# Layer 1 of a four-layer block: the input projected once per pixel and read back in tiles, and two sets of banks for the spreads

## The reference

```python
x_proj = x_nhwc @ w_in + b_in                       # 64 -> 64 channels, per pixel
x1 = gelu(layernorm(depthwise_conv3x3(x)))
offset = x1 @ w_off + b_off                         # 4 groups x 9 taps x 2
mask = softmax((x1 @ w_mask + b_mask), per group over the 9 taps)
out = sum over taps of mask * bilinear_sample(zero_padded(x_proj), tap position + offset)
out = out @ w_out + b_out
y = batch_norm(out);  x = x + y * sigmoid(y)
```

## Time and profile before

| | us |
|---|---|
| median of 3 runs | 1361.74 (1361.45 to 1363.02) |
| the profiled execution, whole | 1360.48 |
| its span, first to last instruction | 1358.7 |
| window_weights, from its first operation to the first transpose | 108.1 to 176.0 |
| transposes of pair 0 | 176.0 to 185.0 |
| spread phase, pair 0 | 185.0 to 220.5 |
| sums phase, pair 0 | 220.5 to 242.8 |
| spread phase, pair 1 | 242.8 to 281.7 |
| sums phase, pair 1 | 281.7 to 299.9 |

### The profile page before, as it was taken

The page is one execution under the profiler, slowest core; times in us unless marked ns, Lnnn a source line. Parts: engine busy times, 40 slices in busy tenths (PEclk is TensorE's granted clock), DMA queues, the critical chain, the costliest instruction groups (busy, mean ns, idle before and its releaser), DMA issues. The chain is left out here.

```text
span 1358.7 us, 31661 instructions
## 1 busy us (share of the span) xinstructions
PE 1114.5 (82%) x13352; PEld 602.8 (44%) x13352; DVE 890.2 (66%) x1220; ACT 645.3 (47%) x1096; POOL 663.2 (49%) x503
## 2 busy tenths in 40 slices
PE   3970099978859999999999576799999999998658
PEld 2440077754315666666666333233333333334323
DVE  3788945566956666667666379646666666667623
ACT  1656035353636677677666343144444444445410
POOL 2000011103345767767764330188888888888600
PEclk9985599898958999999999799699999999999869
DMA  4100000001234555555554005000000000002002
GB/s 87 23 1 0 0 3 3 1 11 43 53 112 141 166 156 163 164 155 160 169 155 117 2 0 140 1 1 2 1 1 2 2 1 2 1 2 80 1 18 71
DMA packets 41841, 75.15 MB, mean 55 GB/s; under 512 B 20876, under 2 KB 26093, under 8 KB 40925
## 3 DMA queue, kind: packets, MB, share of 16 engines
q1 hardware_dynamic: 41533, 72.77, 18.9%
q10 hardware_dynamic: 160, 0.30, 0.1%
HBM read 60.73 MB, written 9.33 MB: 52 GB/s over the span
## 5 line engine op out<-in xcount | busy, mean ns | idle before, releaser
L2264 POOL TENSOR_TENSOR arena_sb<-arena_sb 128x768 f32<-128x768 f32 x168 | 323.0, 1923 | 120.4 <-ACT arena_sb L2225 100.5
L2225 ACT ACTIVATE arena_sb<-ps 128x768 f32<-128x768 f32 x216 | 174.9, 811 | 242.6 <-PE ps L2154 239.4
L2279 DVE TENSOR_REDUCE arena_sb<-ps 128x4 f32<-128x1536 f32 x108 | 188.2, 1757 | 129.4 <-PE ps L2121 128.6
L2154 PE MATMUL ps<-arena_sb 33*64 33x384 f32 x1728 | 187.5, 502 | 11.4 <-ACT arena_sb L2225 5.5
L2166 PE MATMUL ps<-arena_sb 64*64 64x384 f32 x1728 | 168.1, 488 | 3.4 <-ACT arena_sb L2232 3.4
L1633 PE MATMUL ps<-arena_sb 120*64 120x216 f32 x1536 | 166.3, 356 | 0.6 <-DVE arena_sb L1757 0.6
L1783 POOL TENSOR_SCALAR xp_sb<-xp_sb 128x384 f32<-128x384 f32 x69 | 103.0, 1493 | 93.5 <-ACT xp_sb L1682 91.6
L1752 DVE TENSOR_TENSOR arena_sb<-ps,arena_sb 120x384 f32<-120x384 f32 x216 | 119.9, 555 | 2.5 <-ACT arena_sb L1689 2.5
L2121 PE MATMUL ps<-arena_sb 32*128 32x384 f32 x864 | 104.6, 557 | 20.7 <-DVE arena_sb L2279 14.7
L1633 PEld LDWEIGHTS ps<-arena_sb 120*64 120x64 f32 x1536 | 102.0, 137 | 41.9 <-ACT xp_sb L1682 15.3
L1699 ACT ACTIVATE xp_sb<-ps 128x432 f32<-128x432 f32 x192 | 102.4, 534 | 28.8 <-PE ps L1633 28.8
(11 more groups left out here) (249 smaller groups left out, 1636.8 us busy)
## 6 DMA issues: line engine op xcount, KB each, us to landing
xn_sb<-far_hats SPq DMA_DIRECT2D x96, 270.0 KB
arena_sb<-far_hats SPq DMA_DIRECT2D x48, 270.0 KB
arena_sb<-pixel_major SPq DMA_DIRECT2D x96, 120.0 KB, 4.0
far_hats<-xp_sb SPq DMA_DIRECT2D x24, 162.0 KB
pixel_major<-arena_sb SPq DMA_DIRECT2D x24, 108.0 KB
x_sb<-in_x SPq DMA_DIRECT2D x4, 576.0 KB, 8.4
arena_sb<-arena_sb SPq DMA_DIRECT2D x8, 288.0 KB, 5.6
xn_sb<-in_W SPq DMA_DIRECT2D x1, 2304.0 KB, 9.4
```

The costliest lines, as they stand in the source:

```text
L2154: mm = pe.matmul(p_scores(g)[64 * i:64 * i + 64, h, :], kp[own, key:key + 64], qp[own, PIX * b2 + CH * ib:PIX * b2 + CH * ib + CH], start= ...
L2225: act.activation(pt[g % SLOTS].rearrange("p (h n) -> p h n", h=2), p_scores(g), ACT.Exp)\
L2264: pool.tensor_tensor(acc, first, pt[g % SLOTS], ALU.add).then_inc(S["pool_added"], 1)
L2279: v.tensor_reduce(part.rearrange("p (a u j) -> p a u j", a=3, u=NB)[:, a, :, jc], p_m(m), AX.X, ALU.max)\
```

## The change

1. In `window_weights`, PE projects each pixel of the padded input once, 8 rows of the image (two images at a time) to a group, 12 groups. For a group, one matmul with a single row lays down the bias (zero outside the image by the new `valid`), and four accumulate the projected pixels, pixels on partitions. ACT copies the bank to one of four stages, SP stores it to a DRAM tensor `proj`, pixel-major, 128 channels (two images) per pixel. The two padding rows above and below are stored as zeros with the other constants in `offsets0`.
2. In `window_sums`, POOL's lines, PE's `windows`, DVE's bias additions and the waits that went with them are gone. SP loads `xw` from `proj` instead, one DMA per tile, 48 per pair: 10 image rows x 12 pixels x 512 bytes onto 120 partitions. For pair 1, the loads of a row of tiles wait until the sums of pair 0 have used that row.
3. `p_b` becomes two sets of four banks, used in turn. Slot s waits for the copies of slots up to s - 2. The second set lies on the banks of `out` and of the transposes, so its first use in pair 1 waits for `gated`.

The diff, its core:

```diff
@@ load_stage
+    for b2 in range(2):
+        for lo in (0, PQ - 2):
+            edge = PQ * (PQ * b2 + lo)
+            load(k["proj"][edge:edge + 2 * PQ, :], k["zero"][0:2 * PQ, 0:128])
@@ window_weights
+    stages = [stage[0:2 * PQ, 512 * i:512 * i + 512] for i in range(4)]
+    GROUPS = [(b2, 2 + 8 * q) for b2 in range(2) for q in range(HH // 8)]
@@ window_weights, scalar, behind its five operations on offsets and masks
+            for n in range(len(GROUPS)):
+                act.wait_ge(S["proj_ps"], n + 1)
+                if n >= 4:
+                    act.wait_ge(S[f"stored{n % 4}"], 16 * (n // 4))
+                act.activation(stages[n % 4], ps[0:2 * PQ, 512 * (n % 4):512 * (n % 4) + 512], ACT.Copy)\
+                    .then_inc(S["proj_out"], 1)
+        @block.sync
+        def _(sp):
+            for n, (b2, y) in enumerate(GROUPS):
+                sp.wait_ge(S["proj_out"], n + 1)
+                first = PQ * (PQ * b2 + y)
+                sp.dma_start(k["proj"][first:first + 8 * PQ, :].rearrange("(q p) c -> p q c", p=2 * PQ),
+                             stages[n % 4].rearrange("p (q c) -> p q c", c=128)).then_inc(S[f"stored{n % 4}"], 16)
+            for i in range(4):
+                sp.wait_ge(S[f"stored{i}"], 16 * len(GROUPS) // 4)
@@ window_weights, tensor, ahead of its wait for "used" and of keep_clock
+            for n, (b2, y) in enumerate(GROUPS):
+                if n >= 4:
+                    pe.wait_ge(S["proj_out"], n - 3)
+                own = ps[0:2 * PQ, 512 * (n % 4):512 * (n % 4) + 512]
+                pe.matmul(own.rearrange("p (n c) -> p n c", c=C), k["valid"][0:1, :],
+                          k["b_in"][0:1, :].unsqueeze(1).to_broadcast([1, 8, C]), start=True, stop=True)
+                for q in range(4):
+                    first = PQ * PQ * b2 + PQ * (y + 2 * q)
+                    mm = pe.matmul(own[:, 128 * q:128 * q + 128], xq[:, first:first + 2 * PQ], k["win"][:, :],
+                                   start=False, stop=True, skip_group_check=True)
+                mm.then_inc(S["proj_ps"], 1)
@@ window_sums
+    LOADS = NTX0 * NTY * 16
-    p_b = ps[0:KV, 0:2048].rearrange("p (g n) -> p g n", g=G)[:, :, 0:PER * 2 * NTY * NTX0]\
-        .rearrange("p g (q n) -> p g q n", q=PER)
+    p_b = [ps[0:KV, 2048 * i:2048 * i + 2048].rearrange("p (g n) -> p g n", g=G)[:, :, 0:PER * 2 * NTY * NTX0]
+           .rearrange("p g (q n) -> p g q n", q=PER) for i in range(2)]
@@ spread(b, s)
                 if s == 0:
                     pe.wait_ge(S["at"], TURNS * (b + 1))
-                    pe.wait_ge(S["mixed"], NTY * b)
+                    if b:
+                        pe.wait_ge(S["mixed"], NTY * b)
+                elif s == 1:
+                    if b:
+                        pe.wait_ge(S["gated"], NTY * b)
                 else:
-                    pe.wait_ge(S["b_act"], SLOTS * b + s)
-                    pe.wait_ge(S["b_dve"], SLOTS * b + s)
+                    pe.wait_ge(S["b_act"], SLOTS * b + s - 1)
+                    pe.wait_ge(S["b_dve"], SLOTS * b + s - 1)
@@ sums(b, ty)
-                    pe.wait_ge(S["xw"], HALVES * (b + 1))
+                    pe.wait_ge(S["xw"], LOADS * (b + 1))
@@ window_sums, tensor
-                    for m in range(HALVES * s // SLOTS, HALVES * (s + 1) // SLOTS):
-                        windows(b, m)
@@ window_sums, vector
-                    for m in range(HALVES * s // SLOTS, HALVES * (s + 1) // SLOTS):
-                        window(b, m)
@@ window_sums, gpsimd: removed as a whole
@@ window_sums, sync: new
+        @block.sync
+        def _(sp):
+            for b in range(2):
+                for ty in range(NTY):
+                    if b:
+                        sp.wait_ge(S["sums"], ty + 1)
+                    rows = k["proj"][PQ * (PQ * b + TH * ty):PQ * (PQ * b + TH * ty + VH), :].rearrange("(y x) c -> y x c", x=PQ)
+                    for t in range(NTX0):
+                        sp.dma_start(xw(ty, t, slice(0, 2)).rearrange("p h c -> p (h c)"), rows[:, TW * t:TW * t + VW, :])\
+                            .then_inc(S["xw"], 16)
+            sp.wait_ge(S["xw"], 2 * LOADS)
```

More of the change, by code:

```diff
@@ L475, with window_weights @@
 W = 5
-def window_weights(nc, k, om, hp, hn, A, spare, tmp):
+def window_weights(nc, k, om, hp, hn, A, spare, tmp, stage):
     ctx = k["ctx"]
     S = {n: signal(k, "ww_" + n) for n in
-         ("exped", "steps", "hats", "sized", "ready", "prod", "used", "cleared")}
+         ("exped", "steps", "hats", "sized", "ready", "prod", "used", "cleared", "proj_ps", "proj_out",
+          "stored0", "stored1", "stored2", "stored3")}
+    ps, xq = k["psum"], k["xproj_flat"]
+    stages = [stage[0:2 * PQ, 512 * i:512 * i + 512] for i in range(4)]
+    GROUPS = [(b2, 2 + 8 * q) for b2 in range(2) for q in range(HH // 8)]
     M = 2 * NT
@@ L625, in _, with window_sums @@
             act.wait_ge(S["out"], 2 * CPI)
-def window_sums(nc, k, A, at, bm, xw, bias, work):
-    ps, xq, x = k["psum"], k["xproj"], k["x"]
+def window_sums(nc, k, A, at, bm, xw, work):
+    ps, x = k["psum"], k["x"]
     S = {n: signal(k, "ws_" + n) for n in
-         ("turned", "at", "spread", "b_act", "b_dve", "lined", "xw_ps", "masked", "xw", "sums", "half", "mixed", "y", "gated",
-          "gate", "added", "moments")}
+         ("turned", "at", "spread", "b_act", "b_dve", "xw", "sums", "half", "mixed", "y", "gated", "gate", "added", "moments")}
     PAIR = 2 * PIX
@@ L685, in spread @@
                         own = slice(32 * g, 32 * g + 32)
-                        mm = pe.matmul(p_b[:, g, q, :], k["emb"][own, lo:lo + KV],
+                        mm = pe.matmul(p_b[s % 2][:, g, q, :], k["emb"][own, lo:lo + KV],
                                        at3[own, :, py:HH:TH, px:WW:TW], start=True, stop=True, skip_group_check=True)
                 mm.then_inc(S["spread"], 1)
[L690 to L699, removed]
             def sums(b, ty):
@@ L785, in _ @@
                 gate(b, NTY - 1)
-        @block.gpsimd
-        def _(pool):
-            pool.wait_ge(S["turned"], TURNS)
+        @block.sync
+        def _(sp):
             for b in range(2):
[L791 to L805, removed]
+                for ty in range(NTY):
[6 more added lines that the diff above has]
+            sp.wait_ge(S["xw"], 2 * LOADS)
         @block.vector
@@ L833, in finish @@
                     .then_inc(S["added"], 1)
[L835 to L838, removed]
-                v.tensor_tensor(xw(ty, slice(side, NTX0, 2), slice(0, 2)),
-                                p_tx[side][0:KV, 0:384].rearrange("p (t h c) -> p t h c", t=3, h=2),
-                                bias[:, side:NTX0:2, :].unsqueeze(2).to_broadcast([KV, 3, 2, C]),
-                                ALU.add).then_inc(S["xw"], 1)
             for b in range(2):
@@ L2534, in program @@
         sb("b_in", [128, C])
-        sb("valid", [KV, 3 * NTX0])
+        sb("valid", [1, 2 * PQ])
         sb("gates0", [128, 2])
@@ L2579, in program @@
             at = nb + M * G * W * W
-            window_weights(nc, k, om0, hp, hn, A, arena[:, at:at + 8], (k["xn"][:, :], k["xp_flat"]))
+            assert at + 8 + 2048 <= xq0
+            window_weights(nc, k, om0, hp, hn, A, arena[:, at:at + 8], (k["xn"][:, :], k["xp_flat"]),
+                           arena[:, at + 8:at + 8 + 2048])
             at += 8
@@ L2586, in program @@
             at += (NTY - fits) * row
[L2587 to L2588 removed]
+            assert at <= xq0
             def xw(ty, t, h):
                 return (low0[:, ty] if ty < fits else high[:, ty - fits])[:, t, h, :]
[L2593 to L2594 removed]
+            window_sums(nc, k, arena[:, nb:nb + M * G * W * W + 8], k["xn"][:, :], arena[0:KV, 0:nb], xw,
+                        arena[:, nb:nb + 8 * BAND])
         with nc.Else():
@@ L2740 @@
     a["emb"] = np.tile((np.arange(32)[:, None] < W * W) & (spot[:, None] == np.arange(EMB + KV)), (4, 1)).astype(f)
-    wy, wx = np.divmod(np.arange(KV), VW)
-    oky = [wy >= 2, wy >= 0, wy < TH + 2]
-    okx = [(TW * t + wx >= 2) & (TW * t + wx < WW + 2) for t in range(NTX0)]
-    a["valid"] = np.stack([y_ & x_ for y_ in oky for x_ in okx], 1).astype(f)
+    a["valid"] = np.tile((np.arange(PQ) >= 2) & (np.arange(PQ) < WW + 2), 2)[None].astype(f)
     a["gates0"] = (np.arange(128)[:, None] // 16 % 2 == np.arange(2)).astype(f)
```

17 lines of the change are left out of this document (3 added, 14 removed).

## The result

The changed kernel takes 1339.16 us (median; 1338.65 to 1340.9) where the kernel before takes 1361.6 beside it: a ratio of 0.9841, 95% interval 0.9821 to 0.9860. It is faster by 22.4 us; the forecast was 34.4 us and 1327.5 us. The time lies in the range given, near its upper end, and outside the 1323 to 1329 us of the forecast itself.

The account below looks back on a forecast made before the run. In the spread phases, PE's own work (2.44 us a slot) and the turn of one bank set (2.76) hid each other. Gains of 16.1 us (pair 0) and 18.3 (pair 1) make 34.4, hence 1327.5 us; range 1323 to 1342.

Parts of the forecast that it names:

- Two chains in a slot: Spread phases: PE's work (2.44 us) and one bank set's turn (2.76) hide each other; removing both gives 1.52 us slots.
- Pair 1: Spread phase of pair 1: from 38.9 us to 20.65, 18.3 us gained, including that the clock's dip does not return.
- The cover in `window_weights`: Projection in window_weights costs nothing: done by 168 at half clock, near 150 at full, while DVE runs to 175.5 us.
- The pitch of the loads: SP's loads in window_sums: one issued every 0.45 us, so pair 0's land ahead of 204.5 and stay hidden.
- the prediction's own formula: Sums of pair 0 lose 48c - 24.5 us at pitch c, those of pair 1 48c - 37.5, where positive.
- backed-up queue: Rival: the 96 loads back up on SP's queue, 1365 us at 1.04 us per issue, 1419 at 1.6; chance 0.05.
- the rival of loads that are late in pair 0: Rival: pitch of 0.55 to 0.8 us loses 1.9 to 13.9 us before pair 0's sums, 1329 to 1342 us; chance 0.18.
- The clock: Rival: the clock falls in a spread phase, 1.93 us instead of 1.59 per spreads, costing 4.1 to 4.9, 1332; chance 0.06.
- The sum: Both spread phases together: 34.4 us gained, against the profiled execution 1326.1 us, against the median 1327.3; stated as 1327.5.
- the two sets don't overlap: Rival: in the spread phases copies and spreads still take turns, slot 2.76 us, 1354 us in all; chance 0.03.
- The price per load: Rival: each load pays its own small-transfer price, pitch 0.8 to 1.0 us; 1351.7 us at 0.9; chance 0.04.
- the part on the number of DMA engines: Loads in window_sums: each gets 10 of 16 DMA engines, 135 GB/s, 21.8 us for 2.95 MB; sum unchanged.

Follow-up runs that it names:

- The square above: Slot of pair 0 in four kernels: one set of banks 2.74 us with 0.92 us of other PE work, 3.09 without; two sets 2.37 and 1.37 to 1.39.
- contig: Changed kernel with each load's source 120 consecutive pixels instead of 10 rows of 12 (not the tile's pixels): 1328.46 us, ratio 0.9769.
- rows15: Changed kernel with each load's source 15 rows of 8 pixels instead of 10 rows of 12 (not the tile's pixels): 1353.13 us, one execution.
- pool_half_r5: Changed kernel with every second load issued by POOL instead of SP: 1324.57 us over five executions, ratio 0.9726; an earlier single execution 1326.39 us.

## Why the prediction was right, and where it was off

**Two chains in a slot.** Right. The square above shows that either part alone leaves the slot at 2.37 us or more, and both bring it to 1.37 to 1.39. The working had 1.52 for PE's own part, read as the time from the first spread to the next instruction of another kind; in a series without other work the 32 matmuls follow each other in 1.39 (16.69 / 12). The two phases gained 2.5 us more, mostly by this: 17.9 instead of 19.5 us to the first possible sums in pair 0, and 19.80 instead of 20.65 in pair 1.

**Pair 1.** Right, at 19.1 us for 18.3, but by luck in part. The third slot starts 4.04 us after the first, for 4.2, and waits for DVE's copy, as told. The forecast's gain counted the dip of the clock in this phase as gone, and it came back, shorter than before:

```profile
244.00:248.00 4.00, 3.26 (x69) 3.12 (x68) 2.58 (x3) 1.62 (x2) 0.00 (x0) 0.69 0.29 81
248.00:252.00 4.00, 4.00 (x99) 3.89 (x96) 2.83 (x3) 2.43 (x3) 0.00 (x0) 0.89 0.27 77
```

The last ten slots take 14.67 us, where 1.39 each would be 13.9. The shorter slots hid this loss of 0.8 us.

**The cover in `window_weights`.** Right. PE's projection lay between 108.5 and 160.7 us at clock 0.50, as the working's slow case had it (to 168), and DVE was as full as before (37.40 us of the stretch in the earlier trace rows); the transposes begin 0.31 us later. SP issued its last store at 161.4. The store took SP 0.301 us, less than the 0.46 assumed.

**The pitch of the loads.** This is the step that failed. It was taken at 0.45 us, between 0.406 and 0.460 of the earlier trace rows, chosen by bytes and number of runs; it is 0.798. By the prediction's own formula that loses 48 x 0.798 - 24.5 = 13.8 us in pair 0; the trace shows 216.30 - 204.76 = 11.5, since the sums begin 1.8 us after the last load is issued, where the formula had 4.0. The row that had been set aside as the upper end, 0.597, was nearer, and still too low: contig, rows15 and the changed kernel show that the form of the source in memory sets the price, 0.411, 0.820 and 0.752 us for the same 60 KB. The trace of the kernel before had this price. Its `far_hats` loads have a broken source too, 10 repeats of 6 rows onto 60 partitions, and 270 KB each:

```profile
L1568 SPq DMA_DIRECT2D xn_sb<-far_hats x96: 741/756/1568, 386.3 to 727.4; - x96
L1568 SPq DMA_DIRECT2D arena_sb<-far_hats x48: 741/742/748, 389.6 to 730.8; - x48
```

The prediction knew them by one slow group of four (6.41 us, 1.6 each) and kept them for its backed-up queue; their median, with four and a half times the bytes, is within 0.01 us of what a load of the changed kernel costs. In pair 1 the formula gives 0.8 us; the trace shows none, the sums there wait 1.10 us for ACT's last copy alone. The case that came is the rival of loads that are late in pair 0, at the top of its span of 0.55 to 0.8. It had a chance of 0.18 against 0.64 for the forecast, and the range held the result only because it reached up to this rival.

**The clock.** The forecast had no sums at the lower clock. In the hole ahead of them the clock came down to 0.50, and the sums phase of pair 0 took 2.3 us longer than before. Not all of this is the hole's: in pool_half_r5 the sums wait for no load and 1.12 us for ACT, the clock falls all the same (0.61 from 204 to 208), and the phase takes 23.62 us (204.96 to 228.58), 1.35 more than before. So some 1.0 of the 2.3 us goes with the late loads; rows15, with a hole of 17.50 us, has a phase of 23.73 (221.61 to 245.34), so even that is not firm. Another 1.6 us lies in the transposes: the clock is 1.00 from 171 us on, earlier than before, so `keep_clock` takes 7.01 us instead of 8.49 (1.00 before only from 174 us on) and ends 2.09 us ahead of the transposes, which begin at 0.65 and take 9.88 instead of 8.26. Of the other kernels some show it and some do not (9.83 in pool_half_r5, 8.26 in pool_half).

**The sum.** 34.4 forecast, less 11.5 (loads), 2.3 (longer sums), 1.6 (transposes) and 0.3 (start of the block), plus 2.5 (shorter slots) is 21.2; the marks show 21.05. The terms are differences of the same marks, so the sum shows that none is missing, and not what caused each.

**The other rivals.** That the two sets don't overlap is excluded by the slots. The clock did not fall in the spread phase of pair 0, which ran at 1.00; in that of pair 1 it fell as told above (a mean of 0.91, as before), for 0.8 us and not 4 to 5; and it fell where one set of banks left PE idle. The price per load was not that of a transfer in series: loads of three tiles move at 219 GB/s. The backed-up queue is the mechanism that came, at 0.8 instead of 1.04 us or more. One reading in the part on the number of DMA engines is of other loads than it says: from 399 to 400 us the 0.24 MB move in 119 packets of 2 KB, the rows of the `pixel_major` loads. The `far_hats` loads move earlier, from 390 to 392 us, with the same share, 0.66, at 207 GB/s. The sum does not hang on it.

## What to carry to other kernels

Where two chains of about the same length hide each other, measure a slot with each of them taken away, and expect the full gain only when both go; taking work off TensorE alone can even lose time, by the clock. Price a new DMA by the issue time of one of the same form on the same queue, broken source and all, and not by its bytes; once 48 of them stand ahead of a wait and nothing hides them, a tenth of a microsecond in the price is five in the sum. Take the median of such a group, and not one group of it. If a queue is full while the DMA engines are at a quarter, hand half of it to an idle queue before anything else.

## What the runs showed of the hardware

- In these runs SP's issue time goes by the source's form more than by bytes: medians of 0.301 us for the stores of 208 KB from 104 partitions, 0.411 for a load from one run of 120 pixels, 0.752 from 10 rows of 12, 0.820 from 15 rows of 8, the last three with 60 KB onto 120 partitions, and 0.742 for 270 KB from 10 repeats of 6 rows. POOL issues the 10 rows of 12 in 0.59 us (median; 0.57 to 0.84).
- Three matmuls that nobody needs, in each slot, made a kernel faster by 1.1%, with the granted clock at 1.00 instead of 0.50.
- In the projection PE was busy 47.22 of 52.20 us at a mean granted clock of 0.50; in pair 1's spread phase it was busy 17.81 of 19.70 us at 0.91. These runs do not tell the cause.
